# Gathering tile 1's value rows into the query heads' buffer, and taking the first score row's maxima block by block, in a three-layer decoder kernel

## What is computed

```
# 1: neuron memory
shared_compress = einsum('bn,ndr->bdr', neuron_w, compress)   # neuron_w: from a scan and a router over all tokens
Q       = einsum('bsd,bdr->bsr', x, shared_compress)
scores  = einsum('bsr,nr->bsn', Q, K) / sqrt(128)             # K: 8192 keys
top, idx = top_k(scores, 8)
x = layernorm(x + einsum('bskd,bsk->bsd', V[idx], softmax(top)))
# 2: cross attention, 16 heads of 64, mask, clip of the logits to [-5, 5]
x = layernorm(x + attention(x @ Wq, ctx @ Wk, ctx @ Wv) @ Wo + bo)
# 3: experts: per group of 32 tokens each expert slot takes the token with the largest logit
x = layernorm(x + experts(x))
```

## Time and profile before

| what | value |
|---|---|
| median of 3 runs | 1360.39 us (1360.38 to 1360.89) |
| the profiled execution's own time | 1361.8 us |
| its span, first to last instruction | 1360.0 us |
| mean granted TensorE clock | 0.991 |
| PE busy | 1315.0 us, 97% |
| DVE busy | 1102.1 us, 81% |
| ACT busy, POOL busy | 729.8 us, 724.7 us |
| chain that ended last | PE 88%, DVE 8% |

### The profile page before, as it was taken

How to read it: one execution, slowest core, us unless ns; L and a number is a source line. 1 busy time by engine, 2 the same in 40 slices (tenths; PEclk the granted TensorE clock), 3 DMA queues, 4 the chain that set the end, 5 groups by cost and what they waited for, 6 DMA issues and landing times.

```text
span 1360.0 us, 25400 instructions
## 1 busy us (share of the span) xinstructions
PE 1315.0 (97%) x9927; PEld 997.2 (73%) x9927; DVE 1102.1 (81%) x1628; ACT 729.8 (54%) x1377; POOL 724.7 (53%) x1009
## 2 busy tenths in 40 slices
PE   8878999999999999999999999999999999999897
PEld 4556777777878787878787878786868686867775
DVE  2389888888888888888888888888888998546567
ACT  1364555555555555555555555555555554336565
POOL 0553565656565656465656464746574746332425
PEclk8999999999999999999999999999999999999999
DMA  9561121212121212121212121212121316002412
GB/s 369 196 199 58 47 75 55 74 56 75 55 75 55 75 54 75 55 75 55 75 54 75 55 75 55 75 55 75 52 77 36 80 38 183 10 17 95 158 37 90
DMA packets 57554, 110.38 MB, mean 81 GB/s; under 512 B 9443, under 2 KB 38107, under 8 KB 56283
## 3 DMA queue, kind: packets, MB, share of 16 engines
q1 hardware_dynamic: 40326, 62.13, 14.9%
q0 software_dynamic: 14848, 41.96, 10.4%
q10 hardware_dynamic: 2260, 4.66, 0.9%
HBM read 98.50 MB, written 10.22 MB: 80 GB/s over the span
## 4 chain that ended last, share of the span: by engine, by line
PE 88%; DVE 8%; issue 1%; POOL 1%; DMA 1%; ACT 1%; SPq 0%; POOLq 0%; DVEq 0%; ACTq 0%
PE side_bank L390 51%; PE score_bank L390 33%; DVE cand_val L1304 2%; DVE cand_idx L1307 2%; PE score_bank L826 2%; DVE x_sum L1330 1%; DVE dispatchedT L1475 1%; PE side_bank L826 1%; POOL v_rows L1537 1%; DVE x L1368 1%; PE side_bank L553 1%; DMA xT_by_step<-in_xTs 0%; PE score_bank L611 0%; POOL exp L1565 0%; DMA shared_compress<-xT_by_step 0%
## 5 line engine op out<-in xcount | busy, mean ns | idle before, releaser
L976 ACT COPY score_row<-score_bank 128x512 f32<-128x512 f32 x512 | 299.2, 588 | 109.6 <-PE score_bank L390 58.9
L1304 DVE MAX8 cand_val<-score_row 128x8 f32<-128x2048 f32 x128 | 291.8, 2280 | 70.6 <-ACT score_row L976 70.6
L1537 POOL DMA_INDIRECT v_rows<-in_V,top_idx x256 | 248.4, 970 | 122.7 <-issue 70.9
L1565 POOL TENSOR_SCALAR exp<-exp,exp_bound 128x256 f32<-128x256 f32 x512 | 245.1, 495 | 97.3 <-ACT exp L988 95.5
L1307 DVE FIND_INDEX8 cand_idx<-cand_val,score_row 128x8 uint32<-128x2048 f32 x128 | 292.5, 2285 | 0.0
L390 PE MATMUL score_bank<-keysT_hi,qT_hi 128*128 128x512 f32 x512 | 215.5, 421 | 13.0 <-ACT score_row L976 11.9
L390 PE MATMUL score_bank<-keysT_hi,qT_lo 128*128 128x512 f32 x512 | 204.0, 398 | 0.0
L390 PE MATMUL score_bank<-keysT_lo,qT_hi 128*128 128x512 f32 x512 | 203.9, 398 | 0.0
L988 ACT ACTIVATE exp<-side_bank 128x512 f32<-128x512 f32 x256 | 139.0, 595 | 88.3 <-PE side_bank L390 88.3
L390 PE MATMUL side_bank<-qT_heads,kT 64*128 64x256 f32 x1024 | 145.2, 402 | 1.3 <-ACT exp L988 1.3
L1330 DVE SCALAR_TENSOR_TENSOR x_sum<-v_rows,top_weight,x_sum 128x256 f32<-128x256 f32 x256 | 130.0, 508 | 9.2
(11 more groups left out here) (200 smaller groups left out, 2303.5 us busy)
## 6 DMA issues: line engine op xcount, KB each, us to landing
kT<-den_scratch SPq DMA_DIRECT2D x62, 256.0 KB, 4.0
f_quads<-in_f POOLq DMA_DIRECT2D x32, 256.0 KB, 3.4
comp_then_wqkv_raw<-in_comp SPq DMA_DIRECT2D x6, 1024.0 KB, 19.2
xT_by_step<-in_xTs SPq DMA_DIRECT2D x4, 1024.0 KB, 8.8
xT_in<-in_xT SPq DMA_DIRECT2D x16, 256.0 KB, 3.0
keysT_raw<-in_KmT ACTq DMA_DIRECT2D x8, 512.0 KB, 20.6
x_sum<-in_x SPq DMA_DIRECT2D x32, 128.0 KB, 2.0
ctxT_in<-in_ctxT SPq DMA_DIRECT2D x16, 256.0 KB, 4.7
```

Of the source, the lines that this page charges most:

```text
L976: nc.scalar.copy(srow[n // PER % 2][:, i * CB:(i + 1) * CB], scb[n % 3]).then_inc(sem("score_evac"), 1)
L1304: own(nc.vector.max(cv[:, tile, cs], srow[g % 2][:, :]))
L1537: pool.indirect_dma_start(out=vg[:, k, :], out_offset=None, in_=V_rows, in_offset=bass.IndirectOffsetOnAxis(ap=i8[:, tile, k:k + 1], axis=0))\
L1565: last = nc.gpsimd.tensor_scalar(ex[i % NEX][:, k, :], ex[i % NEX][:, k, :], ub[:, k, c:c + 1], E_LO, ALU.min, ALU.max)
```

## The change

- The rows of V of batch 0 tile 1 (`in_ramp`) are gathered into `qT_heads`, with a semaphore of their own, and no longer wait for the sum of tile 0.
- On DVE the sum of tile 0 moves from ahead of row 7 to behind the merge of tile 1. `first_sum` now hangs between the maxima and the search of row 9 (before: of row 10) and holds the norm of tile 0, the sum of tile 1, the low part of tile 0, the norm and the low part of tile 1. Row 9's search and all of row 10 come behind it.
- On POOL the reciprocal root of tile 0 moves from ahead of the gather of tile 1 to behind it.
- On PE and ACT the four blocks of row 11 move from ahead of K projections 2 and 3 to behind the query projections 0 and 1, so that eight blocks stand there in a row. The unread products are 20 and 8 instead of 12 and 4.
- The maxima of row 0 are taken in four blocks of 512 as these arrive, into the places of tile 1 in `cand_val`, and then over those 32.
- The unread products ahead of the first shared query are 40 instead of 24.

```diff
-            warm(24, pp[1])
+            warm(40, pp[1])
...
                 x1_transpose(0, 0)
-                for e in range(4):
-                    score(0, e)
                 project(("K", 0, 2), 1, 4 * P, cth, ctl)
                 project(("K", 0, 3), 1, 6 * P, cth, ctl)
-                fill(12)
+                fill(20)
                 x1_transpose(0, 1)
-                fill(4)
+                fill(8)
                 need(pe, "x1_lo", TT)
                 for j in range(2):
                     project(("Q", 0, j), 0, 2 * j * P, x1h, x1l)
-                for e in range(4, 8):
+                for e in range(8):
                     score(0, e)
...
-                need(dve, "score_evac", PER * (g + 1))
-                own(nc.vector.max(cv[:, tile, cs], srow[g % 2][:, :]))
+                if g == 0:
+                    for n in range(PER):
+                        need(dve, "score_evac", n + 1)
+                        last = nc.vector.max(cv[:, 1, 8 * n:8 * n + 8], srow[0][:, n * CB:(n + 1) * CB])
+                    own(last)
+                    own(nc.vector.max(cv[:, 0, cs], cv[:, 1, :]))
+                else:
+                    need(dve, "score_evac", PER * (g + 1))
+                    own(nc.vector.max(cv[:, tile, cs], srow[g % 2][:, :]))
...
             def first_sum():
 
+                value_norm(0, 0)
                 value_sum(0, 1, range(TOPK))
+                x1_lo(0, 0)
                 value_norm(0, 1)
                 x1_lo(0, 1)
...
                 if ks[0] == 0:
-                    need(pool, "sum_done", TT * batch + tile)
+                    if in_ramp(batch, tile):
+                        need(pool, "sc_stored", 16 * 4)
+                    else:
+                        need(pool, "sum_done", TT * batch + tile)
                     need(pool, "idx_done", TT * batch + tile + 1)
+                rows, landed = (qt, "vg_ramp_in") if in_ramp(batch, tile) else (vg, "vg_in")
```

More of the change, by code:

```diff
@@ L250, in need, with in_ramp @@
                 eng.wait_ge(sem(name), v)
+        def in_ramp(batch, tile):
+            return batch == 0 and tile == 1
         def job_bank(key):
@@ L1049, in ramp @@
                 x1_hi(0, 0)
-                for e in range(4):
-                    score_out(0, e)
                 keys_out(0, 2)
@@ L1327, in value_sum @@
                     need(dve, f"xn_in{tile}", 16 * (batch + 1))
-                    need(dve, "vg_in", 16 * TOPK * (TT * batch + tile + 1))
+                    if in_ramp(batch, tile):
+                        need(dve, "vg_ramp_in", 16 * TOPK)
+                    else:
+                        need(dve, "vg_in", 16 * TOPK * max(TT * batch + tile, 1))
+                rows = qt if in_ramp(batch, tile) else vg
                 for k in ks:
-                    own(nc.vector.scalar_tensor_tensor(acc[:, tile, :], vg[:, k, :], w8[:, tile, k:k + 1],
+                    own(nc.vector.scalar_tensor_tensor(acc[:, tile, :], rows[:, k, :], w8[:, tile, k:k + 1],
                                                        acc[:, tile, :], ALU.mult, ALU.add))
@@ L1433, in _ @@
                 select(c, (4, 5))
-                if mid and c:
+                if mid and c > 0:
                     value_sum(m, 0, range(TOPK))
@@ L1443, in _ @@
                     merge(m, 1)
-                    value_norm(m, 0)
+                    if c == -1:
+                        value_sum(m, 0, range(TOPK))
+                    else:
+                        value_norm(m, 0)
                 candidates(c, 5)
@@ L1456, in _ @@
                                                 sp_[i].rearrange("p (a s) -> p a s", s=S), ALU.mult).then_inc(sem("ot_last"), 1)
-                candidates(c, 6)
-                if c == -1:
-                    x1_lo(m, 0)
-                candidates(c, 7, first_sum if c == -1 else None)
+                candidates(c, 6, first_sum if c == -1 else None)
+                candidates(c, 7)
                 select(c, (12, 13))
@@ L1533, in gather @@
                 if ks[0] == 0:
-                    need(pool, "sum_done", TT * batch + tile)
+                    if in_ramp(batch, tile):
+                        need(pool, "sc_stored", 16 * 4)
+                    else:
+                        need(pool, "sum_done", TT * batch + tile)
                     need(pool, "idx_done", TT * batch + tile + 1)
+                rows, landed = (qt, "vg_ramp_in") if in_ramp(batch, tile) else (vg, "vg_in")
                 for k in ks:
-                    pool.indirect_dma_start(out=vg[:, k, :], out_offset=None, in_=V_rows,
+                    pool.indirect_dma_start(out=rows[:, k, :], out_offset=None, in_=V_rows,
                                             in_offset=bass.IndirectOffsetOnAxis(ap=i8[:, tile, k:k + 1], axis=0))\
-                        .then_inc(sem("vg_in"), 16)
+                        .then_inc(sem(landed), 16)
             def rstd1(batch, tile):
@@ L1575, in _ @@
                             .then_inc(sem("ctx_lo"), 1)
-                    if mid and h == 9 and c != 0:
+                    if mid and h == 9 and c > 0:
                         rstd1(m, 0)
@@ L1591, in _ @@
                         gather(m, 1, range(5, TOPK))
+                if c == -1:
+                    rstd1(m, 0)
             job_full(pool, ("WO", B - 1, TT - 1))
```

## The result

| what | before | after |
|---|---|---|
| median of 5 runs | 1360.39 us (1360.32 to 1363.87) | 1367.48 us (1366.19 to 1369.10) |
| ratio, with 95% interval | | 1.0036 (1.0021 to 1.0050) |
| the profiled execution's time, its span | 1361.8, 1360.0 | 1367.98, 1366.1 |
| mean granted clock | 0.991 | 0.994 |

The change makes the kernel slower by 0.2 to 0.5%, with a higher mean clock. 1361.2 was predicted, with a range up to 1363.3.

What follows compares the result with a forecast made beforehand. PE, 97% busy, was taken as the bound, held by DVE until about 142 us. A gain of 3.1, cut to 0.65 by POOL's wait, less 1.5 for half clock, took 1360.39 to 1361.2 us; range 1359.0 to 1363.3.

Steps and rivals of the forecast that it cites:

- Steps 1 and 2: Ramp: sixteen more unread products bring first scores to clock 1.00; with row 0's maxima by blocks, DVE's chain gains 1.7 us.
- Step 3: DVE's new order in the ramp: PE could transpose tile 1 at 133.5 instead of 140.12 us; POOL's side costs nothing.
- The rule weighed there: Tile 0's sum beside POOL's gathers: shared SBUF interfaces could slow its additions by 0.66 us; taken as 0, bound 0.7.
- Step 4: PE between the two transposes: unread products hold tile 1's transposes until 135.0 us; gain up to query projection 2 is 3.1.
- half clock in the K projections: Rival: half clock lasts through the K projections, X = 136.5; 1361.5 us, or 1362.7 with a second fall; chance 0.08.
- slower: Rival: half clock from row 10's last block into fill(20), X = 138.1; 1364.3 us with the later fall; chance 0.08.
- Step 5: Turn 0: POOL's gathers and clips make PE wait 2.5 us at the second half of values(0, 0); gain left 0.65.
- second wait of 0.3: Turn 0, heads 6 and 7: their clips come 0.3 us behind PE, leaving a gain of 0.35.
- Step 6: Behind the wait in turn 0: PE's clock falls to half for 3.4 us, a loss of 1.5.
- +0.85: Predicted net slowdown in us: gain of 0.65 less the clock loss of 1.5, taking 1360.39 to 1361.2.

Runs made afterwards that it cites:

- e15: The changed kernel with 12 and 4 unread products, turn 0's gathers cut 3, 2, 3, turn 14's 5, 1, 2, without the second half: 1365.29 us, ratio 0.9969.
- e16: The changed kernel with 12 and 4 unread products, turn 0's gathers cut 3, 2, 3 and turn 14's cut 5, 1, 2: 1360.64 us, ratio 0.9941.
- e2: The changed kernel with 24 unread products ahead of the first shared query and row 0's maxima over the whole row: ratio 1.0029.
- e9: The kernel before with one more semaphore that no instruction touches: ratio 0.9995.
- e1: The kernel before with only 40 unread products ahead of the first shared query and row 0's maxima by blocks: ratio 0.9997.
- e4: The changed kernel with three gathers ahead of turn 0's clips and five behind those of heads 2 and 3: ratio 1.0013.
- e7: The changed kernel with turn 0's gathers cut: three ahead of the clips, two behind head 3, three behind head 7: ratio 1.0003.
- e5: The kernel before with only the eight gathers of batch 0 tile 1 on a semaphore of their own: 1365.32 us, ratio 1.0012.
- e6: The changed kernel with turn 14's gathers cut 5, 1, 2 instead of all eight ahead of the clips: 1362.6 us, ratio 1.0000.
- e10: The changed kernel itself run again on another chip: 1373.49 us, ratio 1.0031.
- e12: The changed kernel with one more semaphore that no instruction touches: 1373.93 us, ratio 1.0027.
- e14: The kernel of e16 with 15 more unread products in the 3.4 us spell ahead of row 10's last block: 1361.39 us, ratio 0.9941.

## Why the prediction was wrong

Each step in the profiled execution, counted from the preamble's end:

- **Steps 1 and 2, right for the two traces, not for every execution.** Forecast: the search of row 0 1.7 earlier, clock 1.00 on the first scores. Measured: 17.5 before, 15.7 after, clock 1.00, 0.70 a maximum over 512 where I had drawn 0.69. e15 against e16 gives 1.9. But 1.5 of it is the end of a half clock that the kernel before does not have in every execution (e2 and e9 have the search at 16.0 with 24 products), and that a single trace could not tell me. The trace of the change by itself showed 0.1 (77.01 for 77.11), because its preamble was late.
- **Step 3, right.** The norm of tile 1 was to be ready at 73.9 (133.5 - 59.6) and was at 73.9. The rule weighed there (the Trainium skill, GPSIMD Engine Reference, Key points, on the shared SBUF interfaces) was not seen beside gathers: the eight additions took 4.15 while POOL gathered and 4.13 while it stood idle. The price of 0 was right.
- **Step 4, the term that was mis-sized.** X, the start of tile 1's transposes, was to be 75.4 and was 77.2. The unread products took 4.5 as forecast; but the K projections ran from 129.1 to 134.0, 4.9 instead of 3.1, since the half clock lasted to 133.6. On the prediction's scale X was 136.8, next to the rival *half clock in the K projections* (136.5, chance 0.08) and short of the *slower* one (138.1, chance 0.08), whose half clock ran on into the unread products; its argument against was that no stretch in the rows had lasted longer than 3.75. (By the prediction's own 0.213 a pass the former's 24 passes take 5.1 and give 137.0, not 136.5.) Of the eleven traces that have the spell of 3.4, ten have 6.8 us of half clock there, from 1.0 before the spell's end to 1.1 behind it. Nor does it take so long a spell: e1, e4 and e7 have 6.8 us of it at 99 to 113 us, behind spells of no more than 2.9. The longest stretch in a few rows was no bound.
- **Step 5, right.** Wait 2.5 forecast, 2.35 measured, in the place and for the reason forecast; the second wait of 0.3 is there too, in the 2.23 instead of 1.95 for heads 4 to 7. e4 and e7 show the reason.
- **Step 6, wrong, and it hid part of step 4.** The clock held behind that wait in every trace that has it, so the 1.5 were not lost. The stage lost 1.53; with X at 77.2 and no fall the sum gives 1.84 - 0.65 = 1.2 up to the first `values` and 165.47 - 61.28 = 104.19 against 162.6 - 59.62 = 102.98 is 1.2; 0.3 more came with the second wait. My +0.85 came from a gain of 0.65 and a loss of 1.5 that never was. That it has the sign of what the stage cost is luck.
- **The step that failed: turn 14, put at nothing.** The sum said that whatever TensorE reaches earlier or later behind 142 us moves the end by as much, and gave the gathers' own semaphore no term. It moved a delay of 1.4 on POOL to the one turn without slack: 1.76 in this trace (0.4 of it beyond e5's turn 14, with the stretch at half clock), ratio 1.0012 (1.0000 to 1.0023) for it alone in e5, and 2.2 won back by e6. With X at 77.2, the clock kept and turn 14 at nothing the prediction's sum gives 1360.0 + 1.84, about 1361.9, inside its range; with 1.76 more it is 1363.6, outside. Why the first gather of a tile is late at all stays open.
- **The preamble and the expert stage**, 1.66 and 1.14 of the 6.1 us of span, are this run's. Whether they also stand in the medians' 7.1 us can't be said from one trace; on e10's chip the medians are 4.4 apart, and the two shown causes make 3.3 in this trace. On the chips of e1 to e4 and e9 to e12 the share of turn 14 stays open: the loss by the first half (e2 1.0029, e10 1.0031) is there, but the wait that carries it in turn 14 is another.

## What to carry to other kernels

Filling TensorE's waits with products that nobody reads kept its clock here (e14, and the first scores in all twelve traces with 40 products), but their number is then a term on the path: they must end before the operand they wait for, at either clock, and e14 shows that even a well placed fill can be worth nothing where another wait takes it. When a producer gets one row more of work between its last result and the next, follow the queue behind the following consumer too; here POOL's gathers stood ahead of clips with a margin of 0.55, and cutting them in three groups returned it. Compare the traces up to the last turn, not only around the edit: the turn that is built differently from the others is where a small shift elsewhere lands. And take a half clock into a sum only after more than one trace: the same kernel has it in some executions and not in others.

## What the runs showed of the hardware

- Four times in an execution, 56 indirect gathers apart, POOL starts a gather 1.4 or some 0.6 us later than its releaser allows, without a named cause. Letting eight gathers count on a semaphore of their own moved all four by sixteen gathers (e5); an unused semaphore did not (e9, e12).
- Behind the spell of 3.4 us without work ahead of row 10's last block TensorE ran at 1.2 GHz for 6.8 us in ten of eleven traces and for 3.4 us in one (e7); behind the spells of 1.92 and 2.50 in the kernel before it was 3.4 us. With unread products throughout the spell it kept 2.4 GHz (e14). It kept it in e4 too, where the half clock had come twenty microseconds earlier, the work ahead ended late and the spell was 0.56 long.
- The same spell is not followed by the same clock every time. At one of 2.7 to 2.9 us that ends at 99 to 103 us the half clock came within 2 us of its end in nine of the eighteen traces, some 6 us later in two (e1, e4), and not at all in seven. Behind the 2.1 to 2.3 us ahead of the first shared query, with 24 unread products, it came in four traces of six.
- The same kernel took 1362.8, 1368.8, 1369.1 and 1372.8 us (medians) on four chips, and 1360.4 in the runs of the result, so a change of 0.3% is to be read from ratios on one chip alone. The traces on three of the four have a wait for "remote" of 4.4 to 6.0 us ahead of ScalarE's first copy of `v` in each of turns 0 to 13, where the other traces have 2.9 put to TensorE, and take 2.5 to 5.8 us longer over turns 1 to 13.
